# Half of the first weight tile cast and multiplied before its identity is added, the zero warm-up taken from a constant, and one subtraction of the batch loop moved

## The reference, cut to what matters

```python
def _L0_cond_ref(x, labeler_index, W, lora_A, lora_B_w):      # x: (8, 256, 1024)
    base = jnp.einsum('bsi,oi->bso', x, W)
    low = jnp.einsum('bsi,bir->bsr', x, lora_A[labeler_index])   # R = 32
    return base + jnp.einsum('bsr,or->bso', low, lora_B_w) * 0.5

def _L1_cond_ref(x, adapter_mapping, W, b, lora_As, lora_Bs):
    base_out = jnp.einsum('bti,oi->bto', x, W) + b
    lora_h = jnp.einsum('bti,bir->btr', x, lora_As[adapter_mapping])   # R = 16
    return base_out + jnp.einsum('btr,bro->bto', lora_h, lora_Bs[adapter_mapping]) * 2.0

x = x + _L0_cond_ref(x, itok_B_0_2, L0_cond_W, L0_cond_lora_A, L0_cond_lora_B_w)
x = x + _L1_cond_ref(x, itok_B_0_23, L1_cond_W, L1_cond_b, L1_cond_lora_As, L1_cond_lora_Bs)
```

## Time and profile before

| what | value |
|---|---|
| median of three executions | 295.1 us |
| the profiled execution | 295.05 us, span 293.3 us |
| PE busy | 288.7 us, 98% of the span |
| DVE busy | 243.3 us, 83% |
| ACT busy | 153.5 us, 52% |
| POOL busy | 30.9 us, 11% |
| PE's share of the chain that ended last | 97% |

### The profile page before, as it was taken

How to read it: one execution, slowest core, us unless ns; L and a number is a source line. 1 busy time by engine, 2 the same in 40 slices (tenths; PEclk the granted TensorE clock), 3 DMA queues, 4 the chain that set the end, 5 groups by cost and what they waited for, 6 DMA issues and landing times.

```text
span 293.3 us, 4452 instructions
## 1 busy us (share of the span) xinstructions
PE 288.7 (98%) x1335; PEld 236.1 (81%) x1335; DVE 243.3 (83%) x369; ACT 153.5 (52%) x270; POOL 30.9 (11%) x81
## 2 busy tenths in 40 slices
PE   7999999999999999999999999999999999999996
PEld 6888888888888888877878878878878878878875
DVE  3779997999999999999996797797798698695432
ACT  3574576879257537463553463373364355355120
POOL 0715600010000501000100100100100100100000
PEclk9999999999999999999999999999999999999999
DMA  5999620800006510094167076068068159013004
GB/s 178 321 296 318 107 38 7 139 1 2 0 0 109 98 27 1 6 150 149 29 114 203 22 125 192 17 104 218 4 109 210 16 101 233 6 36 144 0 1 145
DMA packets 100803, 29.17 MB, mean 99 GB/s; under 512 B 85548, under 2 KB 93996, under 8 KB 100788
## 3 DMA queue, kind: packets, MB, share of 16 engines
q1 hardware_dynamic: 100788, 28.99, 42.4%
HBM read 20.59 MB, written 8.39 MB: 99 GB/s over the span
## 4 chain that ended last, share of the span: by engine, by line
PE 97%; DMA 1%; DVE 0%; SPq 0%; issue 0%
PE bank L1200 93%; PE bank L1223 2%; DMA a<-in_L_cond_W 1%; PE bank L1445 1%; PE bank L1412 0%; SPq L273 0%; DVE y L719 0%; DVE a_hi L760 0%; DVE a L719 0%
## 5 line engine op out<-in xcount | busy, mean ns | idle before, releaser
L1200 PE MATMUL bank<-v_hi,lhs 128*128 128x512 f32 (+1 forms) x136 | 42.6, 378 | 0.0
L1200 PE MATMUL bank<-vt_hi,s_hi 128*128 128x512 f32 x96 | 37.3, 389 | 0.0
L1200 PE MATMUL bank<-vt_lo,s_hi 128*128 128x512 f32 x96 | 37.3, 389 | 0.0
L1200 PE MATMUL bank<-vt_hi,s_lo 128*128 128x512 f32 x96 | 37.3, 389 | 0.0
L967 DVE STREAM_TRANSPOSE xt<-raw 128x512 int32<-128x512 int32 x32 | 32.5, 1077 | 0.5 <-DMA raw<-in_x 0.4
L1200 PEld LDWEIGHTS bank<-v_hi,lhs 128*128 128x128 f32 x136 | 25.1, 188 | 4.8
L469 ACT ACTIVATE lhs<-xt 128x512 fp32r<-128x512 f32 x32 | 19.6, 626 | 13.0 <-PE bank L1200 12.7
L1200 PE MATMUL bank<-v_lo,lhs 128*128 128x512 f32 (+1 forms) x68 | 25.8, 380 | 0.0
L1200 PE MATMUL bank<-vt_hi,lhs 128*128 128x512 f32 x64 | 22.1, 406 | 0.0
L719 DVE TENSOR_TENSOR lhs<-xt,lhs 128x512 fp32r<-128x512 f32 x32 | 21.7, 686 | 0.3
L435 POOL CAST ac<-c_hi 128x128 fp32r (+1 forms) x16 | 7.2, 450 | 135.9 <-PE bank L1200 98.9
(11 more groups left out here) (170 smaller groups left out, 658.0 us busy)
## 6 DMA issues: line engine op xcount, KB each, us to landing
raw<-in_x SPq DMA_DIRECT2D x32, 256.0 KB, 4.9
out<-y SPq DMA_DIRECT2D x31, 256.0 KB, 2.6
n<-in_L_cond_W SPq DMA_DIRECT2D x16, 256.0 KB, 5.8
a<-in_L_cond_W SPq DMA_DIRECT2D x16, 256.0 KB, 5.1
a_raw<-in_L_cond_lora_A SPq DMA_DIRECT2D x8, 128.0 KB, 2.4
b_raw<-in_L_cond_lora_Bs SPq DMA_DIRECT2D x16, 64.0 KB, 2.1
e_raw<-in_L_cond_lora_Bs SPq DMA_DIRECT2D x32, 32.0 KB, 1.8
a_raw<-in_L_cond_lora_As SPq DMA_DIRECT2D x8, 64.0 KB, 2.5
```

What stands on the lines that cost most here:

```text
L1200: return nc.tensor.matmul(ps, lhsT, rhs, start=start, stop=stop, skip_group_check=more)
```

## The change

Three things change.

1. The warm-up. `blank`, its memset on DVE and its semaphore are gone (the addresses behind it move down by 512 bytes). PE multiplies a zero constant instead, 128 weight columns by 64 moving columns, six times instead of four; the constant is float32, not fp32r, and POOL writes it before the barrier at the program's start. Seven transposes of `eye` follow instead of eight. The five behind `turn_b11(0)` stay.
2. The first tile of W0. DVE casts the half with columns 256 to 511, which the identity doesn't touch, before it adds eye; then it adds eye and casts the other half. PE multiplies the parts m = 2, 3, 0, 1 in this order, and m = 2 waits for the first cast, m = 0 for the second.
3. `a_low(b + 1, 3)` is made at the end of batch b instead of at the start of batch b + 1: in the loop behind the last output sum, in batch 0 ahead of the output sums.

```diff
-            nc.vector.memset(blank[:, :].bitcast(F32), 0.0).then_inc(blank_made, 1)
             dve.wait_ge(eye_steps, 2)
             dve.wait_ge(n11_in[0], 16)
             tt(n11[:, 0, 0, :], n11[:, 0, 0, :], eye[:, :], ALU.add, n_eyed)
+            def a11_high(j, cols):
+                nc.vector.tensor_copy(a11_hi[:, j, cols], a11[:, j, cols]).then_inc(w0_hi_made, 1)
+
             for j in range(2):
+                dve.wait_ge(a11_in[j], 16)
+                if j == 0:
+                    a11_high(0, sides[1])
                 part = a11[:, j, P * j:P * j + P]
-                dve.wait_ge(a11_in[j], 16)
                 tt(part, part, eye[:, :], ALU.add, w0_eyed)
                 dve.wait_ge(w0_eyed, j + 1)
-                for part in sides if j == 0 else (slice(0, H),):
-                    nc.vector.tensor_copy(a11_hi[:, j, part], a11[:, j, part]).then_inc(w0_hi_made, 1)
+                a11_high(j, slice(0, H) if j else sides[0])
                 b11_low(j)
                 a11_low(j)
...
             def batch(b, first, final):
-                if not first:
-                    a_low(b, 3)
-                    if not final:
-                        dve.wait_ge(s_sum_made, 4 * b + 4)
-                        turn_next(b + 1, range(3))
+                if not (first or final):
+                    dve.wait_ge(s_sum_made, 4 * b + 4)
+                    turn_next(b + 1, range(3))
...
+                if first:
+                    a_low(b + 1, 3)
                 quarter_out(C22, BANK_E, z_sum)
                 quarter_out(C12, BANK_C, u2_sum)
                 if not final:
                     s_low(b + 1, 3)
                 quarter_out(C21, BANK_D, u2_sum)
+                if not (first or final):
+                    a_low(b + 1, 3)
...
-                for m in range(HK):
+                for m in (2, 3, 0, 1) if j == 0 else range(HK):
+
                     if j == 0 and m in (0, 2):
-                        pe.wait_ge(w0_hi_made, 1 + m // 2)
+                        pe.wait_ge(w0_hi_made, 2 - m // 2)
                     mm(LOW[m][:, :], row_tile(a11_hi, j, m), b11_hi[:, j, :], j == 0, False)
...
-            pe.wait_ge(blank_made, 1)
-            for n in range(4):
-                mm(Q_BANK[0][:, P * n:P * n + P], blank[:, :], blank[:, :], True, True)
+
+            zeros = nc.const_aps.tensor_like(0.0, eye[:, :])
+            for n in range(6):
+                mm(Q_BANK[0][:, 64 * n:64 * n + 64], zeros, zeros[:, 0:64], True, True)
             pe.wait_ge(eye_steps, 2)
-            warm_up(8)
+            warm_up(7)
```

More of the change, by code:

```diff
@@ L35, in two_layer_lora_kernel @@
     EYE = 23 * SLOT
-    BLANK = EYE + P * 4
-    INDEX = BLANK + P * 4
+    INDEX = EYE + P * 4
     B0A1 = INDEX + 256
@@ L106, in two_layer_lora_kernel @@
     eye = at("eye", [P, P], F32, EYE)
-    blank = at("blank", [P, P], F32R, BLANK)
     index = at("index", [1, 2 * B], I32, INDEX)
@@ L171, in two_layer_lora_kernel @@
         y_out = [sem(f"y_out{n}") for n in range(4)]
-        index_steps, blank_made = sem("index_steps"), sem("blank_made")
+        index_steps = sem("index_steps")
         eye_steps = sem("eye_steps")
```

## The result

The changed kernel takes 296.53 us (median of 7 runs, 296.08 to 296.69), the kernel before 295.1 us in the same measurement (7 runs, 294.92 to 296.1). The ratio is 1.0033 with a 95% interval of 1.0018 to 1.0048: slower by some 1.4 us. The forecast was 294.7 us, in a range up to 295.6. The profiled execution of the changed kernel took 296.53 us itself, that of before 295.05, so the two traces lie 1.48 us apart and can be compared step by step.

What follows compares the result with a forecast made beforehand. PE was taken to bound the kernel (97% of the chain), leaving gains only ahead of 5.82 us and in pauses between matmuls. Terms 0 - 0.12 - 0.19 = -0.31 took 295.05 to 294.7 us, range 294.3 to 295.6.

Steps and rivals of the forecast that it cites:

- The warm-up, term 0 with ends of 0 and +0.20: Kernel start: zero products at 0.23 us each, turn of n11 still at 3.74, so no gain or loss.
- the first rival: Warm-up: zero products take 0.42 us each, first product some 0.2 us late, 295.06 us in all; chance 17%.
- The new warm-up begins earlier and has six products in place of four: Warm-up: the prediction's argument against TensorE reaching 2.4 GHz only behind the first eight products.
- the late clock: First products: 2.4 GHz granted only behind the first eight, 296.8 us; chance 8% beyond the bound, 3% below it.
- The earlier start: Warm-up: PE waits for the program's barrier alone and starts at 0.85 us instead of 1.11.
- The first tile, -0.12: First a11 tile: first product 0.32 us earlier, at 5.50, of which 0.12 lasts; ends of 0 and -0.32.
- the cap by DVE's s_lo: PE's load around 41 us waits for s2's low part: 41.07 instead of 41.19, only 0.12 us remain.
- The cap by b_lo at 6.69: First products: b11_lo, ready at 6.47, lets PE go on at 6.69 against 6.82; of 0.32 us, 0.13 remain.
- The margin of 0.05 at b11_hi: First product at 5.50: its other operand is ready at 5.31, with 0.05 us to spare after 0.14.
- a rival: One gain alone: a small-margin wait eats the front's gain, or other waits replace part 3's; 294.9 us, 18%.
- Part 3 of x, -0.19: Start of `u_product` in sample 1: PE's wait for part 3 goes, step 0.23; ends of 0 and -0.19.
- The sum: Whole kernel: 0 - 0.12 - 0.19 = -0.31 us, from 295.05 to 294.74.

Runs made afterwards that it cites:

- fourteen transposes: Changed kernel with four blank products and fourteen transposes ahead of the turn of n11 as its warm-up: 295.77 us, ratio 1.0001 [0.9989, 1.0013] against the kernel before.
- eleven blanks: Changed kernel with eleven fp32r blank products of 128 columns and seven transposes as its warm-up: 296.19 us, ratio 1.0025 [1.0014, 1.0037] against the kernel before.
- six wide zeros: Changed kernel with six fp32r zero products of 512 columns and one transpose as its warm-up: 295.34 us, ratio 0.9996 [0.998, 1.0011] against the kernel before.
- transposes alone: Changed kernel without zero products, eight transposes of eye as its warm-up: 296.01 us, ratio 1.001 [0.9993, 1.0026] against the kernel before.
- four fp32r constants: Changed kernel with four zero products from the constant read as fp32r, 128 columns, and eight transposes: 295.08 us, ratio 0.9977 [0.9961, 0.9994].
- first tile alone: Kernel before with only the first tile's cast and products reordered: 295.48 us, ratio 0.9991 [0.9974, 1.0007].
- part 3 alone: Kernel before with only part 3 of x moved: 295.11 us, ratio 0.998 [0.9964, 0.9995].

## Why the prediction was wrong, by its own steps

- **The warm-up, term 0 with ends of 0 and +0.20: this step failed**, in its size and in what it left out. The zero product was taken at 0.23, the nearest row; it measured 0.43, the upper bound of 0.42 and a little more, since each is two records of 0.215. So the first rival's condition held, and by its working the first product would have come at 5.99 (6.02 by its own terms, since 4.4 + 2.2 x 0.11 is 4.64, not 4.61) and the kernel taken 295.06. It came at 6.69. That working took over the clock's rise at 4.4 from before. With the steps of 0.215 instead of 0.11 until then, and then four products at 0.43 instead of 0.25 (1.70 us for 1.00), the loss is 0.87 ahead of the first product and 0.70 in the first four, 1.57 in all, where the rival had 0.17. Measured in place of the term: +1.57, between two single profiles, of which that of before has the earliest rise of all fourteen. By the rival's working the length alone, with the rise at 4.4, would be 0.17 of it, and the later clock 1.40. Between medians the late turn and the later clock came out about even (fourteen transposes and eleven blanks, above).
- **"The new warm-up begins earlier and has six products in place of four"**, the argument against the late clock, was not borne out. More short zero products went with a later rise, not an earlier one, in the pair of eleven blanks and fourteen transposes. The late clock was priced for the first eight products (296.8); it was the first four and the transposes ahead of them. It was treated as independent of the slow products, and the two came together.
- **The earlier start**: 0.83 measured, 0.85 forecast.
- **The first tile, -0.12**: nothing of it can show in the changed kernel. a_hi's first half was ready at 4.77 + 0.29 = 5.06, 1.6 us before PE's first product, which waited for b11_hi instead (6.01 + 0.60, then 0.08). And the load at 41 us came at 42.76, 0.83 behind the end of s2's low part. Done alone, its profile ends 290.49 - 290.28 = 0.21 earlier; the cap by DVE's s_lo was seen at 41.03 (forecast 41.07). The cap by b_lo at 6.69 was not: those products started at 6.48. b11_lo, which was to stay where it was, was itself ready 0.12 earlier (6.35 for 6.47). The margin of 0.05 at b11_hi was used up, as a rival had it, and cost 0.09: the product starts at 5.45, 0.05 behind ACT's end, in place of 5.36 (4.93 + 0.29 + 0.14). The median alone (0.9991 [0.9974, 1.0007]) can't tell this gain from none.
- **Part 3 of x, -0.19**: right, in place and size. The step is 0.23, the seven take 1.75, and the loss shrinks from 1.58 at 43 us to 1.39 at the end. Done alone, 0.998 [0.9964, 0.9995]: a gain that is clear of none, and 0.19 us (0.9994) lies within the interval, near its end. Its profile ends only 0.13 earlier than that of before, though the first product started 0.21 earlier; the low part of s2 came 0.22 later there, so that the load at 41 us stood 0.10 later than before (41.29 for 41.19).
- **The sum**: with +1.57 in place of 0, 0 in place of -0.12 and -0.19 it is +1.38, against 1.39 between the traces' ends and 1.48 between their times. Part 3 and the cap on the first tile were worked out well, and they were the small terms. That the sum closes leans on the first profile of before; by the medians of the later measurements the new warm-up costs about 1.0 us.

What stays open: why more short zero products ahead go with a later rise. The runs leave out plain float32 as its cause (eleven blanks), the late turn alone (fourteen transposes) and zeros as such (six wide ones). They don't tell whether the short products hold the rise back or merely don't bring it on: with six plain ones or eleven blanks the first transpose also starts later, at 3.41 and 3.52 against 2.02. With six wide zeros it starts at 3.52 too and the rise came at 6.9, but there wide products stand in the place of the short ones; no run leaves that stretch empty. How much is chance in a single profile can't be told from one or two of each; it is the medians that separate the groups. The Trainium skill, "TensorE: Matmul & The Clock Gate", Part 4, has it that transposes don't earn the full clock. The fourteen transposes speak against it: TensorE ran nothing but transposes from 2.02 on, and the pace doubled within the last five of them, ahead of the first product. The profile of transposes alone looks more like the rule: there it doubled only behind eight products. But PE had paused, and the spans of that kernel, 292.9 to 295.1 with a median of 293.4, say that most executions went better.

The two best kernels measured are the rest of the change with the old warm-up (0.9976 [0.9959, 0.9992]) and with four fp32r constants (0.9977 [0.9961, 0.9994]): 0.4 to 0.5 us below the kernel before in the same measurement, and over 1 us below the changed one. The forecast's 0.31 would have fitted either.

## What to carry to other kernels

An instruction kind that no row shows need not be near its nearest row: price it at both bounds, and then follow the worse one through every later step, the clock's among them, since what is late there is late together. A gain of tenths at a cover's edge (the cast here) is gone as soon as another operand is late, while a stall with its own rows (part 3) was priced to the hundredth. Where one kernel's time and span part, as with the transposes alone, look at both before a clock or a wait is blamed. When the start of a kernel is touched, compare medians and the distance between starts, since a single profile holds a clock and landings that another run doesn't have.

## What the hardware showed that was not expected

- A float32 matmul of 64 columns was two loads and two products, 0.43 us at 1.2 GHz; in fp32r 128 columns were one of each, 0.22. The Trainium skill, "FP8 and Floating Point Precision", TensorE Precision Notes, speaks of four passes. The estimate from them was 0.21, if the load hides behind the product; the measurement is twice that. Whether the passes or the two loads make the difference, no run here separates.
- The moment at which TensorE goes from 1.2 to 2.4 GHz differs between executions of one program: about 4.4 us and 5.8 to 6.5 us for before, about 8.2 and 7.4 us for the changed kernel. The landing of a tile differs too: the load of a11 took 3.74 or 4.39 us, and in the two profiles of before, 0.96 us apart, 0.65 of that is the landing and nothing the clock.
- PE's load started 0.05 behind the end of what released it, in each of these places: behind DVE with the first tile alone (41.03 behind 40.98) and with part 3 alone (41.29 behind 41.24), behind ACT with the first tile alone (5.45 behind 5.40).
- The time outside the span is not the same for all kernels: 1.70 to 1.80 us for before, 1.74 to 3.21 with transposes alone, 1.73 to 3.02 with the six wide zeros. What makes it is open.
